# Routing of the second layer's switch experts straight from the normalised rows, with encoder and switch matrices multiplied once on the chip

## The reference

```
x_enc = xt @ enc_w + enc_b                       # 192 -> 64
route_prob = softmax(x_enc @ sw_w + sw_b)        # 64 -> 8
route_prob_max = max(route_prob)
onehot = one_hot(argmax(route_prob))
h = gelu(einsum('td,edr->ter', xt, w1) + b1) * onehot
out = (einsum('ter,erd->td', h, w2) + onehot @ b2) * route_prob_max
```

## Time and profile before

| | |
|---|---|
| median of 3 runs | 512.55 us (511.44 to 514.87) |
| the profiled execution | 507.84 us, span 506.1 us |
| mean granted TensorE clock | 0.936 of full speed |
| TensorE busy | 444.0 us, 88% of the span |
| VectorE busy | 271.2 us, 54% |
| ScalarE busy | 206.1 us, 41% |
| share of the chain that ended last | PE 70%, DVE 10%, ACT 8%, issue 6% |

### The profile page before, as it was taken

One profiled execution on the slowest core, in us unless ns is written; L12 is line 12 of the kernel. 1 busy time (PEld: TensorE's weight loads), 2 busy tenths in 40 slices (PEclk: granted clock), 3 DMA queues, 4 the chain that ended last, 5 costly groups with the idle time before them and its releaser, 6 DMA issues.

```text
span 506.1 us, 11503 instructions
## 1 busy us (share of the span) xinstructions
PE 444.0 (88%) x3886; PEld 367.7 (73%) x3887; DVE 271.2 (54%) x917; ACT 206.1 (41%) x424; POOL 91.1 (18%) x117
## 2 busy tenths in 40 slices
PE   5989999965359999999999939887998999999886
PEld 5778786855259999999999936655767666676744
DVE  7264766844524445454454548387585562744711
ACT  1323344531114435354353511463683276268140
POOL 1010507263531131221312211001000000000000
PEclk9888999955569999999999979999999999999999
DMA  7980951410122121121212144000000000000000
GB/s 248 321 355 6 352 198 38 138 51 25 59 83 50 29 65 37 40 58 37 71 32 52 51 125 147 1 1 2 3 2 26 1 3 0 26 3 1 1 24 26
DMA packets 29720, 35.27 MB, mean 70 GB/s; under 512 B 9274, under 2 KB 24890, under 8 KB 29686
## 3 DMA queue, kind: packets, MB, share of 16 engines
q1 hardware_dynamic: 26038, 29.47, 18.7%
q0 software_dynamic: 3072, 4.95, 2.9%
q10 hardware_dynamic: 576, 0.40, 0.2%
HBM read 27.04 MB, written 9.14 MB: 71 GB/s over the span
## 4 chain that ended last, share of the span: by engine, by line
PE 70%; DVE 10%; ACT 8%; issue 6%; POOL 3%; DMA 2%; DVEq 1%; POOLq 0%; ACTq 0%; SPq 0%
PE ps L826 12%; PE ps L794 9%; PE ps L667 7%; PE ps L853 5%; PE ps L805 5%; PE ps L974 4%; PE ps L647 3%; PE ps L962 3%; PE ps L865 2%; PE ps L894 2%; PE ps L698 2%; PE ps L879 2%; PE ps L929 2%; DVE x_tok L1334 2%; POOL xs_dram L595 1%
## 5 line engine op out<-in xcount | busy, mean ns | idle before, releaser
L826 PE MATMUL ps<-w,hidT 128*128 x384 | 65.1, 326 | 0.0
L826 PEld LDWEIGHTS ps<-w,hidT 128*128 128x128 f32 x384 | 62.0, 190 | 0.0
L625 POOL DMA_INDIRECT ys_dram<-ys,y_place_now x32 | 31.2, 975 | 119.0 <-DVE ys L1570 114.1
L794 PE MATMUL ps<-xsT,low_now 128*128 128x128 f32 x384 | 50.8, 282 | 0.2 <-ACT xsT L1101 0.2
L1125 ACT ACTIVATE hidT<-ps,b_act_now 128x128 f32<-128x128 f32 x96 | 28.2, 364 | 53.8 <-issue 51.5
L794 PEld LDWEIGHTS ps<-xsT,low_now 128*128 128x128 f32 x384 | 45.3, 191 | 5.5 <-issue 3.1
L583 POOL TENSOR_TENSOR rstd<-meanvar,eps 128x4 f32<-128x4 f32 (+1 forms) x18 | 3.6, 202 | 240.2 <-DVE meanvar L1327 135.6
L667 PE MATMUL ps<-w_tok,patches 128*128 128x192 f32 x192 | 41.0, 376 | 5.5 <-DMA patches<-in_patches 5.5
L667 PEld LDWEIGHTS ps<-w_tok,patches 128*128 128x128 f32 x192 | 38.4, 227 | 6.3 <-issue 6.0
L1555 DVE TENSOR_SCALAR hidT<-ps,b_dve_now 128x128 f32<-128x128 f32 x96 | 27.7, 344 | 25.4 <-PE ps L805 25.4
L595 POOL DMA_INDIRECT xs_dram<-x_tok,rows x32 | 34.1, 1066 | 23.8 <-DVE rows L1462 15.4
(11 more groups left out here) (208 smaller groups left out, 790.9 us busy)
## 6 DMA issues: line engine op xcount, KB each, us to landing
patches<-in_patches SPq DMA_DIRECT2D x6, 768.0 KB, 5.9
w<-in_W SPq DMA_DIRECT2D x8, 576.0 KB
xs<-xs_dram SPq DMA_DIRECT2D x36, 96.0 KB
w_low<-in_W_low SPq DMA_DIRECT2D x8, 384.0 KB
patches<-in_patches SPq DMA_DIRECT2D x4, 384.0 KB, 4.0
w_high<-in_W_high SPq DMA_DIRECT2D x8, 192.0 KB
y_first<-ys_dram SPq DMA_DIRECT2D x4, 384.0 KB, 3.5
y_second<-ys_dram SPq DMA_DIRECT2D x4, 384.0 KB, 4.2
```

The source lines that it names most:

```text
L625: nc.gpsimd.indirect_dma_start(out=ys_dram[:, :], out_offset=bass.IndirectOffsetOnAxis(ap=y_place_now[v][:, 0:1], axis=0), in_=ys[v][:, :] ...
L794: mm = pe.matmul(ps[:, 4 + 2 * v + m // 3, P * (m % 3):P * (m % 3) + P], low_now[v][:, P * m:P * m + P], xsT[v][:, 0, :], start=(starts an ...
L826: mm = pe.matmul(ps[:, 2 * v + 1, 0:D], hidT[v][:, m, :], w2[:, bass.ds(experts[v], 1), D * m:D * m + D].rearrange("p e n -> p (e n)"), st ...
```

## The change

The product of encoder and switch matrices, with the encoder's bias carried as one more column, is made once on TensorE (`switch_weights`, two products of 8 columns into PSUM bank 6) and copied by VectorE into a new tile `switch_w`. From then on the logits of a chunk are eight products of 8 columns (two per tile) whose stationary operand is the transposed normalised rows `xT`; row 96 of `xT`'s first half, which is 1.0 throughout, brings the bias. `encode`, ScalarE's `encoded`, the tile `xeT` and its two memsets go away; `enc_w` and `enc_b` are replaced by one load `enc_t`. In the loop `switch_logits` takes the place of `encode`, ahead of `scores(c, 1)`; at the end it stands directly behind `turn`, with the three `hidden` parts behind it. `switch_weights` is queued on TensorE ahead of `turn(2, 0, 0, 1)`, behind the 20 identity products and the waits for late weights. VectorE waits for it, and makes its two copies, ahead of `add_experts(0)`. TensorE waits for the copies before it uses bank 6 again.

```diff
@@ tiles
-        enc_w = sb("enc_w", [FG, 2, R1])
-        enc_b = sb("enc_b", [R1, 1])
+        enc_t = sb("enc_t", [R1 + 1, D + 1])
+        switch_w = sb("switch_w", [FG + 1, 2, E])
...
-        xeT = sb("xeT", [R1 + 1, CW])
@@ late_loads
-            (enc_w[:, :, :], A["enc_w"]), (enc_b[:, :], A["enc_b"]), (sw_w[:, :], A["sw"]),
+            (enc_t[:, :], A["enc_t"]), (sw_w[:, :], A["sw"]),
@@ tensor
-                def encode(c):
-
-                    for g in range(2):
-                        group_there(3, c + 1, g)
-                        mm = pe.matmul(ps[0:R1, FFN[c][2], 0:CT], enc_w[:, g, :], seqs(xT[1][0:FG, g, :]),
-                                       start=(g == 0), stop=(g == 1))
-                    mm.then_inc(enc_in_psum, 1)
+                def switch_weights():
+
+                    pe.matmul(ps[0:FG + 1, 6, 0:E], enc_t[:, 0:FG + 1], sw_w[:, :], start=True, stop=True)
+                    pe.matmul(ps[0:FG, 6, E:2 * E], enc_t[:, FG + 1:D + 1], sw_w[:, :], start=True, stop=True
+                              ).then_inc(switch_in_psum, 1)
 
                 def switch_logits(c):
 
-                    pe.wait_ge(enc_done, c + 1)
+                    pe.wait_ge(switch_done, 1)
                     for i in range(TILES):
-                        mm = pe.matmul(ps[:, FFN[c][3], E * i:E * i + E], xeT[:, P * i:P * i + P], sw_w[:, :],
-                                       start=True, stop=True)
+                        for g in range(2):
+                            if i == 0:
+                                group_there(3, c + 1, g)
+                            k = FG + 1 - g
+                            mm = pe.matmul(ps[:, FFN[c][3], E * i:E * i + E], xT[1][0:k, g, P * i:P * i + P],
+                                           switch_w[0:k, g, :], start=(g == 0), stop=(g == 1))
                     mm.then_inc(s_logits_in_psum, 1)
...
+                switch_weights()
                 turn(2, 0, 0, 1)
-                queries_keys(0, range(HG))
+                queries_keys(0, range(2))
+                pe.wait_ge(switch_done, 1)
+                queries_keys(0, range(2, HG))
...
                     scores(c, 0)
                     if later_ffn:
-                        encode(c - 1)
+                        switch_logits(c - 1)
                     scores(c, 1)
                     if later_ffn:
-                        switch_logits(c - 1)
                         hidden(c - 1, 0, range(3))
...
                 turn(3, 1, FFN[c][0], CHUNKS)
-                encode(c)
-                hidden(c, 0, range(2))
                 switch_logits(c)
-                hidden(c, 0, [2])
+                hidden(c, 0, range(3))
@@ scalar
-                def encoded(c):
-
-                    act.wait_ge(enc_in_psum, c + 1)
-                    if c:
-                        act.wait_ge(s_logits_in_psum, c)
-                    nc.scalar.activation(seqs(xeT[0:R1, :]), packed(ps[0:R1, FFN[c][2], 0:CT]), ACT.Identity,
-                                         bias=enc_b[:, 0:1]).then_inc(enc_done, 1)
-
...
                     square(c, 0)
-                    if c:
-                        encoded(c - 1)
                     square(c, 1)
...
                 turned(3, 1, FFN[c][0], CHUNKS)
-                encoded(c)
                 switch_exp(c)
@@ vector
-                nc.vector.memset(xeT[0:R1, :], 0.0)
-                nc.vector.memset(xeT[R1:R1 + 1, :], 1.0)
                 nc.vector.memset(sc[:, :, T:HALF], 0.0)
...
+                dve.wait_ge(switch_in_psum, 1)
+                nc.vector.tensor_copy(switch_w[0:FG + 1, 0, :], ps[0:FG + 1, 6, 0:E])
+                nc.vector.tensor_copy(switch_w[0:FG, 1, :], ps[0:FG, 6, E:2 * E]).then_inc(switch_done, 1)
                 add_experts(0)
```

More of the change, by code:

```diff
@@ L341, in build @@
         attended = sem("attended")
-        enc_in_psum = sem("enc_in_psum")
-        enc_done = sem("enc_done")
+        switch_in_psum = sem("switch_in_psum")
+        switch_done = sem("switch_done")
         s_logits_in_psum = sem("s_logits_in_psum")
@@ L1838, in _layout @@
     np_["Wv"] = groups(wv.reshape(D, D).T)
-    np_["enc_w"] = groups(L1_ffn_enc_w)
-    np_["enc_b"] = np.asarray(L1_ffn_enc_b).reshape(R1, 1)
+    enc = np.zeros((R1 + 1, D + 1), np.asarray(L1_ffn_enc_w).dtype)
+    enc[0:R1, 0:FG] = np.asarray(L1_ffn_enc_w)[0:FG].T
+    enc[0:R1, FG] = np.asarray(L1_ffn_enc_b)
+    enc[R1, FG] = 1.0
+    enc[0:R1, FG + 1:] = np.asarray(L1_ffn_enc_w)[FG:].T
+    np_["enc_t"] = enc
     np_["sw"] = np.concatenate([np.asarray(L1_ffn_sw_w), np.asarray(L1_ffn_sw_b)[None]], 0)
```

## The result

The changed kernel takes 526.2 us (median of 4 runs, 525.1 to 533.8) where the kernel before took 512.1 in the same comparison: ratio 1.026, 95% interval 1.021 to 1.031. It is slower, as forecast, but by 14.1 us by the medians and 13.2 by the ratio, not by 7.75, and it lies above the range (516.3 to 523.5).

A forecast was written before the change was run, and what follows sets the result against it. The prediction took TensorE, busy 88% of the span, and a chain of single engines at layer two's head as the bound; 7.35 + 1.9 - 0.7 - 0.8 = +7.75 us on 512.55 gave 520.3 us, range 516.3 to 523.5.

The forecast's parts named there:

- the loop: Three chunks of layer two: TensorE's work falls 0.51 us per chunk, ScalarE limits the gain to 0.2 each; -0.7 us.
- the end: Last chunk: routing is no longer late, and `turned_choice` follows three hidden parts at 486.25 instead of 487.08; -0.8 us.
- The signs that the prediction gave for the head: Layer two's start: VectorE's first row released at about 308.6, TensorE idle over 7 us before `turn`, clock 0.50 at `turn`.
- `square(c, 2)` directly behind the root: Sign in the loop: ScalarE's second square starts behind the root with no wait, at 455.45 instead of 455.68.
- the stretch to the end: Sign: from the end of the queries to the end of the kernel, about 1.5 us shorter than before.
- The head's wait: Layer two's start: VectorE's first row waits behind identity and switch products; 7.35 us later, between 7.2 and 7.6.
- The head's clock: Layer two's start: TensorE idles 7.7 us, so `turn` and first queries run at the lower clock; 1.9 us, 1.4 to 2.4.
- Rival (a): At the head, the clock doesn't fall or comes back at once; +5.85 us, 518.4 us; 10%.
- Rival (b): The clock stays down through the first chunk's queries and keys; +8.3 us instead of 1.9, 526.7 us; 6%.
- (c): At the head, switch products finish before the first rows land, so VectorE isn't held; 511 us, not slower; 4%.
- (d): Products of this shape are cheaper than gate products; loop and end give 3 us rather than 1.5, 518.8 us; 5%.
- The edits at nothing: Dropped memsets of `xeT`, one load fewer, TensorE's second wait for the copies and `switch_done` in the loop; no cost.

The follow-up runs named there:

- wait_only: The kernel before with only two products of the same shape and VectorE's two copies added at the same queue places; 520.7 us, 9.1 above the kernel before.
- early_products: The changed kernel with the two switch products moved ahead of TensorE's wait for the first rows; 518.7 us, 7.0 above the kernel before by the medians.
- after_wide: The changed kernel with its own head and the logits records widened with zeros from 8 to 128 columns; 513.0 us beside 506.5 for the kernel before.
- after_warm: The changed kernel with 28 more identity products between the switch products and `turn`; from `turn` to the values 9.54 us, its one execution no faster as a whole.
- wide_128: early_products with `switch_w` filled with zeros so that each logits record streams 128 columns instead of 8; 510.6 us beside 511.7 for the kernel before.

## Why the prediction was wrong

The step that failed is the loop, and with it the end: the prediction priced the new narrow records by their own time and left out what the granted clock would do behind them. It forecast -1.5 us for the two together; they measured +5.3. The direction was right, and not by luck: it came from VectorE queued behind the identity products, which the runs bear out. The signs that the prediction gave for the head all came true, and so did `square(c, 2)` directly behind the root; the stretch to the end, which should have become about 1.5 us shorter, didn't.

- **The head's wait**, 7.35 us forecast, measured 7.33. wait_only put it into a kernel without anything else and got 7.7; early_products took it out, and it was gone. Over the five profiles with this head it lies between 6.8 and 8.1 us. That 7.33 falls so near to 7.35 is in part luck: the identity products took 6.85 us in this execution instead of 6.28, the two new products and copies only 0.53 (312.66 to 313.19) instead of 0.95, and the way from VectorE's first row to `turn` 7.08 instead of 7.27.
- **The head's clock**, 1.9 us, between 1.4 and 2.4: measured 1.44 in the changed kernel, 1.4 in its second profile (10.85 against 9.50), 1.7 in wait_only and 2.76 in after_wide. after_warm shows the cause as forecast. Rival (a) didn't occur in any of these. One of the three readings under the term is off: the window 28 to 29 at 0.68 puts the clock's return at 28.6 and not 28.3; the term stays 1.9 us with it.
- **The loop**, -0.7 us: measured +4.5. It priced the sixteen logits records at 1.97 us, which they take (1.95), and their followers, the hidden parts, at the 2.12 us of the trace before. The prediction looked for what the records cost while they run and not for what their small width does to the clock of what comes behind. It read the earlier trace rows as full speed nearly everywhere in layer two, and didn't follow up the 8s of layer one, where the clock falls with TensorE busy (86 to 90, above). It counted encode as pure cost, 1.49 us; whether that dense product among narrow ones kept the clock up is a guess that no run tests. Where the clock stayed up the step was right in direction and too cautious: from the values of chunk 1 to the last copy wide_128 takes 485.00 - 358.98 = 126.02 us and the kernel before 481.47 - 354.38 = 127.09, so -1.1 us and not -0.7.
- **The end**, -0.8 us: measured +0.8, for the same reason: the clock was at 0.50 for 3.4 us from 501 on; with 128 columns it is 23.70 instead of 24.63, -0.9.
- **The range** counted the clock only at the head, as an idle engine's matter. The sum without dips, 7.35 + 1.4 - 1.1 - 0.9 = 6.8 us, is near what after_wide shows (6.5 by the medians, 1.4% or 6.9 by the ratio). The dips are the rest: 14.0 - 6.8 = 7 us, of which by the stretches 4.5 + 1.1 = 5.6 lie in the loop and 0.8 + 0.9 = 1.7 at the end. But 1.7 of the loop's share is the dip in chunk 0 (42.50 us from the values to the next `turn` where it was 40.81), as in wait_only, and its cause is open. So the narrow records answer for some 5.7 us in this profile.
- **Rival (b)**, the clock down through the queries, came near the measured time (526.7) for a reason that the trace doesn't bear out: the queries were cold for some 2 us only. **(c)** is what early_products makes true, and with 8 columns even that is slower than before. **(d)**, cheaper records, didn't occur: they took 1.95 us, as priced.
- **The edits at nothing** cost nothing that shows: VectorE's idle time in front of the memset behind the DMA grew from 1.26 to 2.52 us, and landing to `turn` in early_products is 7.34 us.

The Trainium skill, "TensorE: Matmul & The Clock Gate", Part 1, says that the clock is set "based on how busy the PE has been recently". That would let one expect no fall here, if busy is read as the profile's busy share, which was 1.00 in every window around 378. The runs show that this reading is wrong: with the same number of records, 8 columns had 13 dips at 20 places (the five profiles with the new 8-column logits), 128 columns none at 12.

## What to carry to other kernels

Ask of products that replace others not only what they cost but what TensorE's clock does behind them: here rows of 8-column products that looked like a saving slowed down their neighbours by some 5.7 us. Where narrow records take the same time with more columns, try filling them up; 128 instead of 8 cost 0.1 us per sixteen records and gave back 8.1 us by the medians, 4.7 by the ratios. Look at the clock line wherever it isn't 9 while TensorE is busy, also far from the edit. And before a small set-up product is put into a queue, look at what stands in front of it in that queue: a wait for it at the head of another engine inherits all of it, the work whose result nobody reads included.

## What the runs showed of the hardware

- The granted clock fell from 2.4 to 1.2 GHz while TensorE was at 100% of busy time, behind sixteen records with 8 columns (0.50 from about 378.6 to 382 in the changed kernel), at 13 of 20 places in layer two, and at none of 12 with 128 columns. Of the 13 dips seven lasted about 3.4 us and six about 6.8, with TensorE at work. It also fell at full busy time behind products with 400 columns (86.7 to 90.1 in the kernel before); so narrow columns aren't the only thing behind which it falls.
- A record with a stationary tile of 97 x 128 in fp32 takes 0.12 us with 8, 32 or 128 moving columns (1.95, 1.97 and 2.05 us for sixteen).
- The dips aren't at the same places in every kernel: chunks 1 and 3 in the changed one, in both its profiles, chunk 1, chunks 1 and 2 or chunk 3 in others, and always at the end. Kernels that have them spread more in time: ten runs of the 8-column kernel with the early products lie within 10.8 us, ten of the 128-column one within 3.4.
